# Row maximum subtracted on VectorE instead of GpSimd in a Swin block fused with a convolution block

## The chip, the cores and the metric

The kernel runs on one core of one Trainium2 chip. The metric is the device time of one launch in microseconds (us), the median of several runs. The engines of the core are TensorE (PE in the profile), VectorE (DVE), ScalarE (ACT), GpSimd (POOL) and SyncE (SP), which only issues DMAs here. Each works through its own instruction list in order; they meet through semaphores.

## The reference

Sixteen images of 128 channels x 32 x 32 pass through two blocks, all in float32. The first is a Swin block on 8x8 windows with 8 heads of 16 channels:

```
t    = layernorm(tokens)                    # per token, over 128 channels
q, k, v = t @ qkv_w.T + qkv_b               # 16 windows x 64 tokens, 8 heads
attn = softmax(q * scale @ k^T + bias)      # per window and head, 64 x 64, over the keys
tok  = tok + (attn @ v) @ proj_w.T + proj_b
out  = tok + gelu(layernorm(tok) @ w1.T + b1) @ w2.T + b2
```

The second is a convolution block on the output of the first: a 1x1 convolution with gelu, dilated row and column convolutions with 3x3 convolutions behind them, a pyramid of grouped 3x3 convolutions, an edge gate, a branch of 2D Fourier transforms, a softmax over five routes that mixes the branches, relu and a last 1x1 convolution.

The change concerns the softmax of the first block: `exp(s - max(s)) / sum`, where the maximum is over the 64 keys of one query and head.

## The kernel before

One call of `both(n, n+1)` on every engine computes the convolution block of image n and the Swin block of image n+1, interleaved. It is run 15 times: once for images 0 and 1, then 14 times in a loop. Ahead of it stands the Swin block of image 0 alone (`swin_rest(0)` on VectorE, `swin_only(0)` on GpSimd), behind it the convolution block of image 15 alone (`conv_only`). Nothing plans the order: it is the order of calls in each engine's list.

The attention of an image is done in 8 window pairs j = 0..7 (`PAIRS`). A pair's scores are a tile of 128 partitions (2 windows x 64 queries) by 512 columns (8 heads x 64 keys), in one of three `score` buffers. A pair goes through these steps:

1. PE, `scores` (L518): four matmuls per pair into PSUM bank 2 or 3.
2. DVE, `bias_max`: L957 adds the relative position bias and writes `score` to SBUF, L959 is a drain (wait until the engine's own work is written), L960 finds the 8 row maxima.
3. POOL, `less_max` (L1666): waits for the semaphore `s_max`, subtracts the maxima from `score` in place, 128x512, and signals `s_sub`.
4. ACT, `exponent` (L1382): waits for `s_sub`, exponential in place.
5. DVE, `row_sums`: L964 sums, L966 takes the reciprocal; POOL, `widen_inverse` (L1677), spreads the 8 inverse sums over 128 columns. PE, `prob_transposes` (L529), ACT, `prob_copy` (L1387), PE, `values` (L540).

On VectorE pair j+2 is prepared before pair j is summed, and a slot of convolution work follows each pair:

```
                bias_max(i, 0)
                route_logits(n)
                bias_max(i, 1)
                for j in range(PAIRS):
                    if j + 2 < PAIRS:
                        bias_max(i, j + 2)
                    row_sums(i, j)
```

So of the 8 calls of `bias_max`, two stand ahead of the loop and six in its passes j = 0 to 5. The convolution slots hold: j = 0 `mix_input` (L1129, L1131), j = 1 `odd_part` (L1032 to L1039), j = 2 and 3 taps (L1088, L1090) and the bias L1099, j = 4 `boosted` (L1108, L1113), j = 5 `even_product` (L1117), `odd_product` (L1124) and a tap, j = 6 `gate_pyramid` (L1139) and taps. In the pass j = 5 TensorE does `inverse_even` (L467, 16 matmul records), which waits for L1117, and then `pyramid_conv` (L647, 48 records), for which L1139 waits. All 8 calls of `bias_max` stand ahead of L1117 in VectorE's list.

GpSimd in `both` does `axis_conv` (L1696, L1706, L1708: taps of the row and column convolutions, with two of them in the passes j = 0 and 1), `residual_in` (L1660), `less_max`, `widen_inverse` and two additions at the end.

Of the kernel before, what the change touches and what calls it, by code (L numbers as in the profile page):

```python
# [27 lines left out]
ALU = mybir.AluOpType  # L28
ACT = mybir.ActivationFunctionType
AX = mybir.AxisListType  # L30
# [3 lines left out]
P = 128  # L34
CH = TOK // P
HALF = TOK // 2
WS, HEADS = 8, 8
WT = WS * WS
HD = C // HEADS
WIN = TOK // WT  # L40
PAIRS = WIN // 2
# [99 lines left out]
def swin_conv_kernel(nc, x, cols, rows, mats, cons, rel_index, out):  # L141
    with ExitStack() as ctx:
        def sb(name, *free, dt=F32):
            return ctx.enter_context(nc.sbuf_tensor(name, [P, *free], dt))

        def sem(name):
            return ctx.enter_context(nc.semaphore(name))
# [9 lines left out]
        def col(name, k=0):  # L157
            return cols_sb[:, COLS[name][0] + k:COLS[name][0] + k + 1]
# [40 lines left out]
        score = sb("score", 3, HEADS, WT)  # L199
# [3 lines left out]
        row_max, row_sum, row_inv = sb("row_max", 3, HEADS), sb("row_sum", 3, HEADS), sb("row_inv", PAIRS, HEADS)  # L203
# [52 lines left out]
        pool_turns = sem("pool_turns")  # L256
# [15 lines left out]
        v_sb = sem("v_sb")  # L272
        s_ps = sem("s_ps")
        s_biased = sem("s_biased")
        s_max = sem("s_max")
        s_sub = sem("s_sub")
        s_exp = sem("s_exp")
        s_inv = sem("s_inv")
# [85 lines left out]
        def grid(ap):  # L364
            return ap.rearrange("p (h w) -> p h w", w=SIDE)
# [545 lines left out]
        def _(dve):  # L911
# [40 lines left out]
            def bias_max(i, j):  # L952
                dve.wait_ge(s_ps, 8 * i + j + 1)
                if j >= 3:

                    dve.wait_ge(pT_ps, 8 * i + j - 2)
                dve.tensor_tensor(score[:, j % 3].rearrange("p h k -> p (h k)"), bank[2 + j % 2][:], rel_bias[:],  # L957
                                  ALU.add).then_inc(s_biased, 1)
                dve.drain()  # L959
                dve.tensor_reduce(row_max[:, j % 3], score[:, j % 3], AX.X, ALU.max).then_inc(s_max, 1)  # L960

            def row_sums(i, j):
                dve.wait_ge(s_exp, 8 * i + j + 1)
# [212 lines left out]
            def swin_rest(i):  # L1176
                keys(i)
# [6 lines that stand above are left out]
                scale_values(i, 0)  # L1184
                residual_stats(i, 0)
                scale_values(i, 1)
                norm2(i, 0)
                residual_stats(i, 1)
                norm2(i, 1)
                swin_out(i, 0)  # L1190
                swin_out(i, 1)
# [444 lines left out]
        @block.gpsimd  # L1636
        def _(pool):

            pool.memset(z_sb[:], 0.0)
            pool.drain()  # L1640
            pool.sem_inc(z_zeroed, 1)
            for padded in (hor, ver, pyr):
                pool.memset(padded[:], 0.0)
            pool.memset(v_pair[:], 0.0)
            pool.wait_ge(onehot_ready, 4)
            pool.memset(k_heads_flat[:, 0:WT * WT], 0.0)
            pool.wait_ge(rel_ps, 2)
            pool.memset(k_heads_flat[:, WT * WT:2 * WT * WT], 0.0)
            pool.drain()
            pool.sem_inc(zeroed, 1)  # L1650
            pool.wait_ge(setup_dve, 1)


            def residual_in(i):
                pool.wait_ge(xT_sb, 2 * i + 2)
                pool.sem_inc(pool_turns)

                pool.wait_ge(x1_sb, 2 * i)
                pool.sem_inc(pool_turns)
                pool.tensor_tensor(resT[:], xT[:], proj_shift[:].unsqueeze(1).broadcast_to([P, CH, C]), ALU.add)\  # L1660
                    .then_inc(res_sb, 1)

            def less_max(i, j):
                pool.wait_ge(s_max, 8 * i + j + 1)
                pool.sem_inc(pool_turns)
                pool.tensor_tensor(score[:, j % 3], score[:, j % 3],  # L1666
                                   row_max[:, j % 3].unsqueeze(2).broadcast_to([P, HEADS, WT]), ALU.subtract)\
                    .then_inc(s_sub, 1)

            def widen_inverse(i, j):  # L1670
                pool.wait_ge(s_inv, 8 * i + j + 1)
                pool.sem_inc(pool_turns)
                if j % 4 == 0:

                    pool.wait_ge(iv_ps, 2 * i)
                    pool.sem_inc(pool_turns)
                pool.tensor_copy(inv_wide[:, j], row_inv[:, j].unsqueeze(2).broadcast_to([P, HEADS, HD]))\  # L1677
                    .then_inc(iv_wide, 1)

            mid = AXIS_TAPS // 2  # L1680
            OFFSETS = [0] + [AXIS_DIL * (t - mid) for t in range(AXIS_TAPS)
                             if t != mid and abs(AXIS_DIL * (t - mid)) < SIDE]

            def axis_conv(n, a, offsets):

                dst, name = ((hor, "dilh"), (ver, "dilv"))[a]
                body = dst[:, 1:1 + SIDE, 1:1 + SIDE]
                for off in offsets:
                    weight = col(name, off // AXIS_DIL + mid)
                    if off == 0:  # L1690
                        pool.wait_ge(act_sb, 2 * n + 2)
                        pool.sem_inc(pool_turns)

                        pool.wait_ge(hv_sb, n)
                        pool.sem_inc(pool_turns)
                        pool.tensor_scalar(body, act_in, weight, 1.0, ALU.mult, ALU.mult)  # L1696
                        continue
                    lo, hi = max(0, -off), min(SIDE, SIDE - off)
                    if a == 0:
                        part = (slice(None), slice(None), slice(lo, hi))  # L1700
                        of = act_in[:, :, lo + off:hi + off]
                    else:
                        part = (slice(None), slice(lo, hi))
                        of = act_in[:, lo + off:hi + off]
                    pool.drain()
                    pool.tensor_scalar(axis_part[part], of, weight, 1.0, ALU.mult, ALU.mult)  # L1706
                    pool.drain()
                    last = pool.tensor_tensor(body[part], body[part], axis_part[part], ALU.add)  # L1708
                    if off == OFFSETS[-1]:
                        last.then_inc(axis_sb, 1)  # L1710

            def mix_pyramid(n):

                pool.wait_ge(py_sb, 2 * n + 2)
                pool.sem_inc(pool_turns)
                pool.wait_ge(xm_mixed, n + 1)
                pool.sem_inc(pool_turns)
                pool.tensor_tensor(py[:], py[:], grid(xm[:]), ALU.add).then_inc(pyramid_mixed, 1)

            def square_sum(n):  # L1720
                pool.wait_ge(be_sb, 2 * n + 2)
                pool.sem_inc(pool_turns)
                pool.wait_ge(bo_sb, 2 * n + 2)
                pool.sem_inc(pool_turns)
                pool.tensor_tensor(fa, fa, fb, ALU.add).then_inc(sq_sb, 1)

            def swin_only(i):
                residual_in(i)
                less_max(i, 0)
                less_max(i, 1)  # L1730
                for j in range(PAIRS):
                    if j + 2 < PAIRS:
                        less_max(i, j + 2)
                    widen_inverse(i, j)

            def both(n, i):
                axis_conv(n, 0, OFFSETS)
                axis_conv(n, 1, OFFSETS[:3])
                residual_in(i)
                less_max(i, 0)  # L1740
                less_max(i, 1)
                for j in range(PAIRS):
                    if j + 2 < PAIRS:
                        less_max(i, j + 2)
                    widen_inverse(i, j)
                    if j < 2:
                        axis_conv(n, 1, OFFSETS[3 + j:4 + j])
                mix_pyramid(n)
                square_sum(n)

            def conv_only(n):
                axis_conv(n, 0, OFFSETS)
                axis_conv(n, 1, OFFSETS)
                mix_pyramid(n)
                square_sum(n)

            swin_only(0)
            both(0, 1)
            with pool.Fori(1, IMAGES - 1) as n:
                both(n, n + 1)  # L1760
            conv_only(IMAGES - 1)
# [81 lines left out]
```

## Time and profile before

| | us |
|---|---|
| Median of 3 runs | 1808.63 (1806.32 to 1815.72) |
| The profiled execution's own time | 1805.41 |
| Its span in the trace | 1803.6 |
| PE busy | 1549.4 (86%) |
| DVE busy | 1364.0 (76%) |
| ACT busy | 864.2 (48%) |
| POOL busy | 684.9 (38%) |

Busy time of an engine is the sum of its instructions' durations; a matmul's end is modelled. Register, branch, semaphore and DMA-issuing instructions are not counted. "PEclk" is the clock that TensorE was granted, as a share of 2.4 GHz: 1.00 is 2.4 GHz, 0.50 is 1.2 GHz. The chain of waits is followed back from the last instruction: at each step to what released it, or to the instruction before it on its engine; "DVEq" is VectorE's queue, mostly its drains.

### The profile page before, as it was taken

Reading aid. Unit: us, or ns where it says so; the run is one execution under the profiler, and the core shown is the slowest. Engines: PE = TensorE matmul, PEld = TensorE weight load, DVE = VectorE, ACT = ScalarE, POOL = GpSimd, SP = SyncE. Lnnn points to the kernel's source line nnn. Section 1 sums busy time; section 2 is a strip of 40 time slices with the busy share of each in tenths; the row PEclk is TensorE's granted clock in tenths of the full one; section 3 lists DMA queues with packets and bytes.
Section 4 is the critical chain, followed back from the end, with each engine's and each line's share of the span. In section 5 each row is a group of like instructions: output and inputs, shape, how many; then the busy total and the mean of one; then the engine's idle time right before and its main releaser. Section 6 shows DMA issues by size and latency. Waiting matters only on the chain.

```text
span 1803.6 us, 32142 instructions
## 1 busy us (share of the span) xinstructions
PE 1549.4 (86%) x11664; PEld 906.3 (50%) x11664; DVE 1364.0 (76%) x2455; ACT 864.2 (48%) x1380; POOL 684.9 (38%) x603
## 2 busy tenths in 40 slices
PE   5789899888989889888998988889888898988884
PEld 3346455464555546445463554546455464555542
DVE  4558778687777878788687777868788786778866
ACT  2344545455454544545455454544545545454533
POOL 3244251634416244251534416134251623416151
PEclk9899999999999999999999999999999999999997
DMA  4011020111102011020111102011020201102020
GB/s 147 1 26 41 26 52 1 43 33 37 39 23 53 0 37 39 25 51 0 43 33 37 39 23 53 0 37 39 25 51 0 58 18 37 39 12 53 0 54 12
DMA packets 19618, 60.23 MB, mean 33 GB/s; under 512 B 6228, under 2 KB 6228, under 8 KB 19204
## 3 DMA queue, kind: packets, MB, share of 16 engines
q1 hardware_dynamic: 19588, 59.83, 13.7%
q8 instruction: 18, 0.29, 0.1%
q14 instruction: 12, 0.10, 0.0%
HBM read 14.04 MB, written 9.02 MB: 13 GB/s over the span
## 4 chain that ended last, share of the span: by engine, by line
DVE 39%; PE 25%; DVEq 16%; issue 7%; ACT 6%; SPq 4%; DMA 3%; ACTq 1%; POOL 0%; POOLq 0%
DVE hv L1090 16%; DVEq L959 7%; DVE nT L929 5%; PE bank L647 5%; PE bank L674 4%; SPq L428 4%; DVE row_max L960 4%; DVEq L965 3%; PE bank L467 3%; PE bank L518 3%; PE bank L489 2%; DMA k_heads<-kC 2%; PE bank L755 2%; DVE score L957 2%; PE bank L577 1%
## 5 line engine op out<-in xcount | busy, mean ns | idle before, releaser
L674 PE MATMUL bank<-act,mats_sb 128*32 128x512 f32 (+11 forms) x2112 | 267.1, 475 | 1.4 <-DVE xs L1026 1.4
L1666 POOL TENSOR_TENSOR score<-score,row_max 128x512 f32<-128x512 f32 x128 | 133.4, 1042 | 306.7 <-DVE row_max L960 305.1
L1350 ACT ACTIVATE fft<-bank 128x512 f32<-128x512 f32 x224 | 168.9, 807 | 125.7 <-PE bank L467 111.8
L1090 DVE SCALAR_TENSOR_TENSOR hv<-hor,mix,hv 128x1024 f32<-128x1024 f32 x128 | 193.8, 1514 | 10.7
L467 PE MATMUL bank<-cons_sb,fft 128*128 128x128 f32 x1280 | 185.4, 306 | 11.8 <-DVE fft L1117 11.8
L1090 DVE SCALAR_TENSOR_TENSOR hv<-ver,mix,hv 128x1024 f32<-128x1024 f32 x144 | 186.9, 1298 | 11.0
L1382 ACT ACTIVATE score<-score 128x512 f32<-128x512 f32 x128 | 80.8, 631 | 225.8 <-POOL score L1666 225.8
L467 PEld LDWEIGHTS bank<-cons_sb,fft 128*128 128x128 f32 x1280 | 172.7, 217 | 31.4 <-DVE fft L1117 17.0
L1677 POOL COPY inv_wide<-row_inv 128x128 f32<-128x128 f32 x128 | 91.8, 717 | 206.7 <-DVE row_inv L966 206.7
L674 PEld LDWEIGHTS bank<-act,mats_sb 128*32 128x32 f32 x2112 | 117.5, 109 | 99.6 <-issue 81.5
L1696 POOL TENSOR_SCALAR hor<-act,cols_sb 128x1024 f32<-128x1024 f32 x16 | 18.0, 1125 | 391.6 <-ACT act L1407 391.6
L518 PE MATMUL bank<-k_heads,qC 128*64 128x512 f32 x512 | 136.1, 621 | 31.8 <-DMA k_heads<-kC 31.8
L577 PE MATMUL bank<-nC,mats_sb 128*128 128x512 f32 x256 | 127.4, 621 | 38.9 <-ACT nC L1350 23.4
L957 DVE TENSOR_TENSOR score<-bank,rel_bias 128x512 f32<-128x512 f32 x128 | 87.2, 681 | 76.3 <-PE bank L518 76.2
L1387 ACT ACTIVATE probT<-bank 128x512 f32<-128x512 f32 x128 | 77.7, 607 | 101.6 <-PE bank L529 101.3
L1706 POOL TENSOR_SCALAR axis_part<-act,cols_sb 128x320 f32<-128x320 f32 (+1 forms) x128 | 109.4, 855 | 22.5 <-issue 22.5
L587 PE MATMUL bank<-fft,mats_sb 128*128 128x512 f32 x256 | 115.2, 593 | 0.0
L1400 ACT ACTIVATE fft<-bank,fold_b 128x512 f32<-128x512 f32 x128 | 79.2, 689 | 68.5 <-PE bank L577 68.5
L929 DVE TENSOR_SCALAR nT<-xT,mv,rstd 128x128 f32<-128x128 f32 x256 | 104.8, 491 | 3.8
L1708 POOL TENSOR_TENSOR ver<-ver,axis_part 128x320 f32<-128x320 f32 (+1 forms) x64 | 100.8, 1575 | 9.4
L960 DVE TENSOR_REDUCE row_max<-score 128x8 f32<-128x512 f32 x128 | 87.8, 686 | 11.6
L577 PEld LDWEIGHTS bank<-nC,mats_sb 128*128 128x128 f32 x256 | 45.1, 191 | 98.2 <-issue 34.4
(180 smaller groups left out, 2903.9 us busy)
## 6 DMA issues: line engine op xcount, KB each, us to landing
pyr_stack<-pyr SPq DMA_DIRECT2D x192, 144.2 KB, 3.1
x_in<-x_dram SPq DMA_DIRECT2D x16, 512.0 KB, 3.5
k_heads<-kC SPq DMA_DIRECT2D x128, 64.0 KB, 2.4
out_dram<-y_out SPq DMA_DIRECT2D x16, 512.0 KB, 2.8
k_heads<-rel_dram SPq DMA_DIRECT2D x2, 1024.0 KB, 13.0
mats_sb<-mats_dram SPq DMA_DIRECT2D x1, 1978.5 KB, 7.4
z_dram<-z_sb SPq DMA_DIRECT2D x32, 19.1 KB
z_run<-z_dram SPq DMA_DIRECT2D x16, 38.2 KB
```

Source lines behind the costliest of these rows:

```text
L467: last = pe.matmul(dst[:, c * P:(c + 1) * P], src[:, at:at + P], rhs, start=True, stop=True)
L518: last = pe.matmul(bank[2 + j % 2][64 * e:64 * e + 64, :], qC[:, w * WT:(w + 1) * WT], k_heads[:, :, w], start=True, stop=True)
L577: pe.matmul(bank[b][:], w_up[:, f * P:(f + 1) * P], nC[:, HALF * k:HALF * k + HALF], start=True, stop=True).then_inc(up_ps, 1)
L587: last = pe.matmul(bank[b][:], w_down[:, f * P:(f + 1) * P], hidden[:, f, HALF * k:HALF * k + HALF], start=False, stop=(f == FC - 1))
L674: last = pe.matmul(grids[32 * d:32 * d + 32, y0 - 16 * k:y1 - 16 * k, x0:x1], w_pyr[:, d, t], act[:, y0 + dy:y1 + dy, x0 + dx:x1 + dx], st ...
L929: last = dve.tensor_scalar(nT[:, c], source[:, c], mv[:, c, 0:1], rstd[:, c:c + 1], ALU.subtract, ALU.mult)
L957: dve.tensor_tensor(score[:, j % 3].rearrange("p h k -> p (h k)"), bank[2 + j % 2][:], rel_bias[:], ALU.add).then_inc(s_biased, 1)
L959: dve.drain()
L960: dve.tensor_reduce(row_max[:, j % 3], score[:, j % 3], AX.X, ALU.max).then_inc(s_max, 1)
L1090: last = dve.scalar_tensor_tensor(hv[:], src, mix[:, a, k:k + 1], hv[:], ALU.mult, ALU.add)
L1350: return act_.activation(dst, src, ACT.Copy)
L1666: pool.tensor_tensor(score[:, j % 3], score[:, j % 3], row_max[:, j % 3].unsqueeze(2).broadcast_to([P, HEADS, WT]), ALU.subtract)\
```

## The change

`bias_max` on VectorE gets a second drain and the subtraction behind the maximum. `less_max` on GpSimd and the semaphore `s_max` go. ScalarE's wait on `s_sub` stays as it is; it is now VectorE that raises it. No DMA, tile or matmul is touched.

```
@@ bias_max (VectorE)
                 dve.drain()
-                dve.tensor_reduce(row_max[:, j % 3], score[:, j % 3], AX.X, ALU.max).then_inc(s_max, 1)
+                dve.tensor_reduce(row_max[:, j % 3], score[:, j % 3], AX.X, ALU.max)
+                dve.drain()
+                dve.tensor_tensor(score[:, j % 3], score[:, j % 3],
+                                  row_max[:, j % 3].unsqueeze(2).broadcast_to([P, HEADS, WT]), ALU.subtract)\
+                   .then_inc(s_sub, 1)
@@ GpSimd
-            def less_max(i, j):
-                pool.wait_ge(s_max, 8 * i + j + 1)
-                pool.sem_inc(pool_turns)
-                pool.tensor_tensor(score[:, j % 3], score[:, j % 3],
-                                   row_max[:, j % 3].unsqueeze(2).broadcast_to([P, HEADS, WT]), ALU.subtract)\
-                    .then_inc(s_sub, 1)
@@ swin_only and both (GpSimd)
                 residual_in(i)
-                less_max(i, 0)
-                less_max(i, 1)
                 for j in range(PAIRS):
-                    if j + 2 < PAIRS:
-                        less_max(i, j + 2)
                     widen_inverse(i, j)
```

## Rows read from the trace of the kernel before

**Rows 1.** The page's chain that ended last, by engine and by line

```profile
DVE 39%; PE 25%; DVEq 16%; issue 7%; ACT 6%; SPq 4%; DMA 3%; ACTq 1%; POOL 0%; POOLq 0%
```

**Rows 2.** The chain in order of time, one attention stage: start us, us, what

```profile
920.65 1.36 DVE fft L1117
922.05 3.78 PE bank L467 x16
...
931.73 0.75 DVE py L1139
```

**Rows 3.** Timeline of DVE, same stage: start us, us, line, operation, [idle before]

```profile
887.72 0.87 DVE L1059 TENSOR_SCALAR route<-route,vec 128x5 f32<-128x5 f32 x1
...
889.27 0.69 DVE L960 TENSOR_REDUCE row_max<-score 128x8 f32<-128x512 f32 x1
892.09 0.69 DVE L957 TENSOR_TENSOR score<-bank,rel_bias 128x512 f32<-128x512 f32 x1 [2.13 <-PE bank L518]
892.87 0.69 DVE L960 TENSOR_REDUCE row_max<-score 128x8 f32<-128x512 f32 x1
893.47 0.68 DVE L964 TENSOR_REDUCE row_sum<-score 128x8 f32<-128x512 f32 x1
...
901.03 2.09 DVE L1032 TENSOR_TENSOR fft<-xs 128x930 f32<-128x930 f32 x1
...
910.62 2.70 DVE L1090 SCALAR_TENSOR_TENSOR hv<-hor,mix,hv 128x1024 f32<-128x1024 f32 x2
```

**Rows 4.** Timeline of POOL, same stage

```profile
919.88 1.04 POOL L1666 TENSOR_TENSOR score<-score,row_max 128x512 f32<-128x512 f32 x1 [2.53 <-DVE row_max L960]
```

**Rows 5.** DVE's groups by line and form: count, busy us, mean ns, idle before

```profile
L957 DVE TENSOR_TENSOR score<-bank,rel_bias 128x512 f32<-128x512 f32 x128 | 87.2, 681 | 76.3 <-PE bank L518 76.2
...
L1139 DVE SCALAR_TENSOR_TENSOR py<-bank,cols_sb,axis_part 128x512 f32<-128x512 f32 x32 | 24.0, 751 | 83.0 <-PE bank L647 83.0
...
L1159 DVE TENSOR_TENSOR hv<-hv,py 128x1024 f32<-128x1024 f32 x16 | 19.6, 1226 | 1.2
```

**Rows 6.** Single lines over the whole run: duration ns min/median/max

```profile
L1117 DVE TENSOR_TENSOR fft<-fft x16: 1226/1343/1348, 162.0 to 1759.1; 128x1024 f32<-128x1024 f32 x16
...
L1032 DVE TENSOR_TENSOR fft<-xs x32: 1859/2104/3014, 119.4 to 1747.2; 128x930 f32<-128x930 f32 x32
```

**Rows 7.** Waits of all engines: us in total, times, longest

```profile
ACT score L1382 <- POOL score L1666: 225.8, 113, 6.4
...
PEld bank L529 <- ACT score L1382: 27.0, 32, 1.8
```

**Rows 8.** Stretches: us, busy (x) of PE, PEld, DVE, ACT, POOL, PEclk, DMA share, GB/s

```profile
892.00:922.00 30.00, 26.72 (x234) 16.18 (x232) 27.96 (x44) 13.53 (x22) 17.27 (x16) 0.97 0.26 59
...
872.00:876.00 4.00, 4.00 (x11) 2.48 (x12) 0.45 (x1) 0.60 (x1) 3.52 (x5) 0.53 0.00 0
...
922.00:926.00 4.00, 3.95 (x20) 3.69 (x24) 3.37 (x5) 2.79 (x4) 0.35 (x2) 0.50 0.00 0
```

**Rows 9.** Timeline of PE behind L1117 in the next image of the loop

```profile
1029.50 3.55 PE L467 MATMUL bank<-cons_sb,fft 128*128 128x128 f32 x16 [1.04 <-DVE fft L1117]
1032.98 5.36 PE L647 MATMUL bank<-pyr_stack,mats_sb 96*32 96x512 f32 x48
...
1038.50 2.05 PE L467 MATMUL bank<-cons_sb,fft 128*128 128x128 f32 x16
```

**Rows 10.** Timeline of DVE, first image, Swin block alone

```profile
58.82 0.69 DVE L957 TENSOR_TENSOR score<-bank,rel_bias 128x512 f32<-128x512 f32 x1 [0.37 <-PE bank L518]
...
61.53 0.69 DVE L957 TENSOR_TENSOR score<-bank,rel_bias 128x512 f32<-128x512 f32 x1 [0.37 <-PE bank L518]
```

**Rows 11.** Timeline of DVE, the wait behind the first normalisation, in two images

```profile
875.55 0.75 DVE L949 TENSOR_SCALAR kC<-bank,fold_b 128x512 f32<-128x512 f32 x1 [3.73 <-PE bank L489]
877.16 0.75 DVE L949 TENSOR_SCALAR kC<-bank,fold_b 128x512 f32<-128x512 f32 x1 [0.86 <-PE bank L489]
...
983.82 1.52 DVE L949 TENSOR_SCALAR kC<-bank,fold_b 128x512 f32<-128x512 f32 x2 [2.33 <-PE bank L489]
```

More of the change, by code:

```diff
@@ L274, in swin_conv_kernel @@
         s_biased = sem("s_biased")
-        s_max = sem("s_max")
         s_sub = sem("s_sub")
@@ L1739, in both @@
                 residual_in(i)
-                less_max(i, 0)
-                less_max(i, 1)
                 for j in range(PAIRS):
-                    if j + 2 < PAIRS:
-                        less_max(i, j + 2)
                     widen_inverse(i, j)
```

## The prediction

> **What bounds the kernel now.** I read the chain that ended last, by engine, first. VectorE stands on it with 39%, its queue (drains behind its own work) with 16%, TensorE with 25%, and GpSimd with 0% [rows 1]. So work goes from an engine that is on no step of the chain to the one that is on most of it. The question is what of VectorE's own list is covered where the new work lands.
>
> For that I read the chain in order of time and the timelines in one pass of the loop, at 885 to 932 us. The reader is to see three parts. (a) Pairs 0 and 1 go through VectorE, which is done with the maximum of pair 1 at 889.27 + 0.69 = 889.96, and then idles 2.13 us until TensorE's scores of pair 2 let L957 start at 892.09 [rows 3]. (b) From 892.09 to L1117 at 920.65 VectorE has no wait for another engine of over 0.3 us: in 892 to 922 its instructions take 27.96 of 30 us, and the rest is the spacing of some 0.08 us at its drains. TensorE is busy 26.72 us of the same 30 and holds 0.97 of the full clock [rows 8]. (c) L1117 ends at 922.0, TensorE starts L467 on it at 922.05, and VectorE's L1139 waits for L647 until 931.73 (the second half; the first started 929.26) [rows 2]; these waits sum to 83.0 us in the run [rows 5]. What is late at L1117 is therefore late at the end of the image, because the chain goes from VectorE to TensorE and back without slack. From this L957 (pair 2, the last one that waits) to L1117 it is 920.65 - 892.09 = 28.56 us [rows 2, 3], and in all 15 passes between 28.4 and 28.6, whatever the clock did elsewhere. VectorE's own list sets this stage.
>
> **The change part by part.** The subtraction on VectorE, with both inputs in SBUF and 128x512 float32, is not in the trace. The nearest rows are L957, the same shape with one input in PSUM, 0.681 us on average, and L1159, both inputs in SBUF at 1024 columns, 1.226 us [rows 5]. Between the two lie 512 columns, (1.226 - 0.681) / 512 = 1.06 ns a column, which leaves 0.14 us fixed: 0.68 to 0.69 us for the new instruction. Lower bound: 0.61, half of L1159, as if nothing were fixed. Upper bound: L1032, whose inputs are read with large strides, takes at least 1.859 us for 930 columns [rows 6], 1.83 ns a column over the fixed 0.14, so 1.09 us if reading one maximum 64 times over were as slow as that. I take 0.69, since the second input is a contiguous stretch of 8 values, and nothing in the trace shows such a rate for a repeated value.
>
> The Trainium skill ("VectorE: DVE Perf Modes", the section on the errata) gives a float32 tensor_tensor add in SBUF as 691 ns at 512 columns; by that page the term would be the same, and no run here shows the exact instruction yet.
>
> It stands behind a drain. L960 to L964, with none between, start 893.47 - 892.87 = 0.60 apart; L957 to L960, with one, start 892.87 - 892.09 = 0.78 apart for a 0.69 instruction [rows 3]. New order: L960, 0.78 to the subtraction, 0.60 to L964; so 1.38 in place of 0.60, which adds 0.78 us a pair (0.70 to 1.18 with the bounds).
>
> Pairs 0 and 1 (part a): 2 x 0.78 = 1.56 us added. L1059, a 128x5 instruction, takes 0.87 us now, since GpSimd's subtraction of pair 0 runs beside it; its neighbour L1057 on as little data takes 0.16. That 0.65 us should come back. Net 0.9 us, against 2.13 us of idle time [rows 3]. Cost nothing, 1.2 us of cover left; at the upper bound 1.7 us, still covered. Were the cover gone it would cost 0.9 us a pass.
>
> Pairs 2 to 7 (part b): 6 x 0.78 = 4.68 us a pass on the path.
>
> What comes back in part b, because GpSimd's 1.04 us subtraction no longer runs beside VectorE: L1117 takes 1.343 as a median and 1.226 at least [rows 6], 0.12 us, and there L1666 runs from 919.88 to 920.92, over L1117's start [rows 4]. L1032 takes 2.09 against 1.86 undisturbed, 0.23 us [rows 3, 6]. The first of the two L1090 at 910.62 gives 0.06 (2.70 for two that take 1.28 each with 0.08 between) [rows 3]. Sum 0.41. The axis taps that GpSimd runs beside j = 0 and 1 shift with the inverse sums that release them and end, by the same shifts, about 0.1 us ahead of the new subtraction; up to 0.1 us a pass of loss if that fails, which I leave in the range.
>
> The Trainium skill ("SBUF — State Buffer", section "SBUF: two separate sides") says that GpSimd and VectorE share one pair of SBUF ports as an exclusive lock, held for a whole instruction, the other fully blocked. By that rule L1117, begun at 920.65 [rows 2], would lose the 0.27 us until 920.92 and not 0.12; taken so at all three places the return would be about 0.95 us a pass in place of 0.41, and the sum some 8 us lower. The trace shows less than half of the rule's price at L1117, and I go by it.
>
> ScalarE's exponential starts earlier by the difference of the hops: GpSimd's 1.04 plus some 0.2 of semaphores against 0.78. ScalarE waits 225.8 us for GpSimd's subtraction, but TensorE waits only 27.0 us for the exponential [rows 7], and VectorE's sums come two pairs later. Worth nothing in part b. GpSimd is free of 133 us of work that was on no step of the chain: nothing.
>
> Part c moves as a whole by 4.68 - 0.41 = 4.27 us. Fifteen passes: 64 us. The first image, alone: pairs follow each other at 61.53 - 58.82 = 2.71 us, of which VectorE idles 0.37 [rows 10], so 2.34 + 0.78 = 3.12 us of VectorE's work a pair exceeds the pace by 0.4; over some five pairs 2 us, between -2 (the shorter hop to the exponential) and +4. The last image has no softmax.
>
> Own time of the profiled execution 1805.4 (span 1803.6) + 64 + 2 = 1871. The median of three runs is 1808.6, 3 above the profiled one, the lowest 1 above; I take +1: 1872 us.
>
> The clock is the term that I can't work out. TensorE is granted 0.50 in 922 to 926 [rows 8], right behind three short waits on VectorE, and L467 then takes 3.78 us, in the next image 3.55, where 16 records take 2.05 at full clock [rows 9]. Over the 15 passes the time from L1117 to the first L1139 comes as 7.8, 9.1 and 8.6 us in turn, mean 8.5. There is a second such place: TensorE idles while VectorE normalises, the clock falls to 0.53 [rows 8], and VectorE then waits 3.73 + 0.86 = 4.59 us instead of 2.33 [rows 11]; that happens in one pass of three. A pass of 112 us and not 108 will meet this otherwise. If the clock never fell at either place: 15 x (1.7 at L467 + 0.5 at L647) + 5 x 2.26 = 44 us less. If it fell at both in every pass, as in the worst now: 15 x 0.6 + 10 x 2.26 = 32 us more. TensorE will idle more in part b, so I don't expect the good end.
>
> **The rivals.** (R1) *The clock turns against it.* VectorE feeds TensorE more slowly, TensorE's waits in part b grow from some 1 us to 1.8, and the clock falls inside the stage, where TensorE has 26.72 us of work in 30 [rows 8] and at half clock becomes the bound for some us. For it: so little reserve. Against: in 892 to 918 it holds 1.00 throughout. Price: the 32 us above, up to 1903; with a drop inside the stage of 1.7 us a pass, 1928. The Trainium skill ("TensorE: Matmul & The Clock Gate", "HAM oscillation — how this bites in real kernels") says that TensorE fed in bursts falls back to half clock again and again; the granted 0.50 behind the waits agrees.
>
> (R2) *The clock turns for it.* The longer pass puts the fall elsewhere, under VectorE's work. Price: 20 to 44 us less, 1828 to 1852.
>
> (R3) *Not slower.* The pace of the stage is not VectorE's work but the way from maximum to exponential to transposes, through GpSimd. The shorter hop would then win, at most the 27.0 us that TensorE waits for the exponential [rows 7], and the subtractions would fill VectorE's waits for scores, 76.2 us in the run [rows 5]: 1778 to 1806. It decides only if VectorE idles in part b for over 0.78 us a pair. Against it: those waits stand at pairs 0 to 2 and in the first image, and in part b there are none.
>
> (R4) *The repeated maximum is read slowly*: 1.09 us each, 6 x 0.40 x 15 = 36 us more, 1908.
>
> **How the numbers follow.** Forecast (1853 to 1888): 72%. R1 above that: 13%. R2 below that: 8%. R4: 4%. R3: 3%. All but R3 are slower. The likeliest case gives 1872; with a part of R1 and R2 the range is 1849 to 1899. A measurement of this kernel tells about 0.5%, 9 us, from no change: faster 0.02, same 0.02, slower 0.96.
>
> **What would show it.** The new line takes 0.69 us, 128 times; L960 to L964 start 1.38 apart; from pair 2's L957 to L1117 it takes 28.56 + 4.27 = 32.8 us in every pass; L957 of pair 2 still waits, for about 1.2 us; L1059 takes under 0.3 us, L1117 1.23; L1139 still waits some 5 us a pass; the last image is unchanged. It is wrong if pair 2's L957 to L1117 grows by less than 3 us, if the new instruction takes over 0.8, or if L1139 waits less by what L1117 is late.

## The result, and the profile after

| | before | after |
|---|---|---|
| Median, us | 1812.18 (4 runs) | 1881.91 (4 runs, 1877.05 to 1885.19) |
| Ratio, 95% interval | | 1.0383 [1.0337, 1.0429] |
| Profiled execution's own time / span, us | 1805.41 / 1803.6 | 1880.26 / 1878.4 |

The change makes the kernel 3.8% slower, 69 us by the ratio. The forecast was 1872 us, 66 above the profiled execution; that execution came out 74.8 us longer in span. Further runs of the kernel before, beside the experiments, brought its median to 1810.8 and 1812.7. The profiled execution of the kernel before, 1805.41 us, is faster than each of its 34 timed ones (1805.9 to 1820.62), while that of the kernel after lies near its median: so some 5 of the 74.8 us come from which executions are compared, and not from the change.

The page of the kernel after: busy time by engine, and the chain that ended last by engine. [rows 1] is the chain before.

```profile
PE 1583.0 (84%) x11664; PEld 927.6 (49%) x11664; DVE 1428.6 (76%) x2583; ACT 863.5 (46%) x1380; POOL 546.8 (29%) x475
...
DVE 41%; PE 27%; DVEq 14%; issue 6%; ACT 6%; SPq 4%; DMA 3%; ACTq 1%
```

GpSimd is 138 us less busy and VectorE 65 us more. GpSimd had 0% of the chain before, so what its relief is worth can only be what it gives back to VectorE's instructions.

The timeline of VectorE after, pairs 0, 1 and 2 of one pass (start us, us, line, operation, idle before); it answers to [rows 3]. L956, L959, L961 and L967 are bias, maximum, the new subtraction and the sum.

```profile
923.79 0.23 DVE L1062 TENSOR_SCALAR route<-route,vec 128x5 f32<-128x5 f32 x1
...
925.47 0.69 DVE L961 TENSOR_TENSOR score<-score,row_max 128x512 f32<-128x512 f32 x1
927.39 0.69 DVE L956 TENSOR_TENSOR score<-bank,rel_bias 128x512 f32<-128x512 f32 x1 [1.23 <-PE bank L517]
928.17 0.69 DVE L959 TENSOR_REDUCE row_max<-score 128x8 f32<-128x512 f32 x1
928.93 0.69 DVE L961 TENSOR_TENSOR score<-score,row_max 128x512 f32<-128x512 f32 x1
929.54 0.68 DVE L967 TENSOR_REDUCE row_sum<-score 128x8 f32<-128x512 f32 x1
...
937.85 1.72 DVE L1035 TENSOR_TENSOR fft<-xs 128x930 f32<-128x930 f32 x1
...
957.72 0.69 DVE L956 TENSOR_TENSOR score<-bank,rel_bias 128x512 f32<-128x512 f32 x1 [0.78 <-PE bank L517]
...
960.91 1.23 DVE L1120 TENSOR_TENSOR fft<-fft 128x1024 f32<-128x1024 f32 x1
```

What to see: maximum to sum now start 929.54 - 928.17 = 1.37 us apart, not 0.60; the wait ahead of pair 2's score has shrunk from 2.13 to 1.23 us; the route instruction L1062 takes 0.23 us and not 0.87; and there is a wait that wasn't there, 0.78 us ahead of pair 7's score at 957.72.

TensorE in the same pass, ahead of that wait and behind it:

```profile
947.56 0.66 PE L528 MATMUL bank<-cons_sb,score 128*128 128x128 f32 x4
951.92 3.75 PE L466 MATMUL bank<-mats_sb,fft 128*128 128x128 f32 x16 [3.70 <-DVE fft L1102]
955.60 0.66 PE L539 MATMUL bank<-probT,v_pair 128*32 128x64 f32 x16
956.18 1.49 PE L517 MATMUL bank<-k_heads,qC 128*64 128x512 f32 x4
...
962.20 3.79 PE L466 MATMUL bank<-cons_sb,fft 128*128 128x128 f32 x16 [2.03 <-DVE fft L1120]
```

The same place in the kernel before:

```profile
914.06 2.02 PE L467 MATMUL bank<-mats_sb,fft 128*128 128x128 f32 x16 [1.28 <-DVE fft L1099]
```

Stretches of the kernel after, with the granted clock (us, busy (x) of PE, PEld, DVE, ACT, POOL, then PEclk, DMA share, GB/s):

```profile
926.00:950.00 24.00, 21.35 (x193) 12.71 (x192) 21.02 (x35) 11.94 (x19) 9.78 (x8) 1.00 0.33 74
950.00:957.00 7.00, 5.08 (x34) 4.20 (x36) 6.61 (x11) 0.63 (x1) 0.29 (x1) 0.52 0.00 0
960.00:967.00 7.00, 4.97 (x26) 3.89 (x28) 5.35 (x8) 4.08 (x6) 1.59 (x2) 0.53 0.00 0
```

VectorE reaches L1102 later, TensorE waits 3.70 us and not 1.28, the clock falls to 1.2 GHz, the 16 records take 3.75 and not 2.02 us, and pair 7's scores (L517) come too late for VectorE. This is so beyond the one pass. In 14 of the 15 passes TensorE waits 3.66 to 3.86 us at L1102 and the 16 records take 2.54 to 3.76 us; in the last pass it waits 2.35 us and they take 2.02, as they do in all 15 passes of the kernel before, behind waits of 1.1 to 1.3 us. Pair 7's score is late, by 0.7 us or more, in the five passes in which they take 3.75 us or more.

The second place where the clock counts is behind the first normalisation. TensorE in two passes of the kernel after, a short and a long one:

```profile
909.43 0.66 PE L458 MATMUL bank<-cons_sb,nT 128*128 128x128 f32 x4 [1.80 <-DVE nT L928]
...
910.45 1.98 PE L488 MATMUL bank<-nC,mats_sb 128*128 128x512 f32 x4
...
1021.81 1.08 PE L458 MATMUL bank<-cons_sb,nT 128*128 128x128 f32 x4 [1.80 <-DVE nT L928]
...
1023.55 3.78 PE L488 MATMUL bank<-nC,mats_sb 128*128 128x512 f32 x4
```

The wait just ahead is 1.80 us in both, so its length alone does not decide. VectorE's wait at kC, which follows, is the long one in 9 passes of 15, where it was in 5.

**Where the 74.8 us are.** From the VectorE timelines of all 15 passes, before against after:

| stretch of a pass | before, us | after, us | over 15 passes |
|---|---|---|---|
| pair 2's score to the even product, passes without a wait at pair 7 | 28.4 to 28.6 | 32.65 to 32.9 | +62.3 (15 x 4.15) |
| the same, what late passes add | none | 5 passes with a wait at pair 7, 0.7 to 1.3; one late through GpSimd, 1.4 | +6.0 |
| pass begin to pair 2's score | 27.7, 28.7 in the first, 29.9 to 30.3 in 5 | 27.7, and 29.7 to 30.3 in 9 | +8.9 |
| even product to first L1142 | 7.7 to 9.1, mean 8.47 | 7.5 to 8.9, mean 8.27 | -3.0 |
| Swin block of the first image | | | +0.9 |

The sum is 75.1 us against 74.8 in span; so 62 us are VectorE's work, some 10 us TensorE's clock (4.6 at pair 7, 8.9 ahead of pair 2, less 3.0), 1.4 GpSimd and 0.9 the first image. The stage's 62 us are there in every trace of a kernel with the six subtractions (32.6 to 33.0 us in its undisturbed passes); the clock's share is less certain. In the profiled executions of the runs with pairs 0 and 1 alone and with nobody subtracting (below), whose medians are that of the kernel before, the wait behind the first normalisation is the long one in 8 and in 7 passes. So part of the step from 5 to 9 can be chance, and by the medians, 69 to 70 us apart, the clock costs nearer 5 us than 10.

The pass that is late through GpSimd shows how the two engines delay each other, and what it costs when the order turns. VectorE's `mix_input` and GpSimd's tap start within 0.05 us of each other in all 15 passes. In the pass of the rows above VectorE comes through undisturbed and GpSimd waits; VectorE, then GpSimd:

```profile
931.27 1.28 DVE L1132 SCALAR_TENSOR_TENSOR xm<-act,mix,xm 128x1024 f32<-128x1024 f32 x1
932.62 2.30 DVE L1134 SCALAR_TENSOR_TENSOR xm<-xs,mix,xm 128x1024 f32<-128x1024 f32 x1
```

```profile
931.24 1.92 POOL L1703 TENSOR_SCALAR axis_part<-act,cols_sb 128x672 f32<-128x672 f32 x1 [0.19 <-issue]
```

In the one late pass, the last of the loop, it is the other way round, and VectorE pays 0.58 + 0.72 us:

```profile
1721.64 1.86 DVE L1132 SCALAR_TENSOR_TENSOR xm<-act,mix,xm 128x1024 f32<-128x1024 f32 x1
1723.58 3.02 DVE L1134 SCALAR_TENSOR_TENSOR xm<-xs,mix,xm 128x1024 f32<-128x1024 f32 x1
```

```profile
1721.60 0.83 POOL L1703 TENSOR_SCALAR axis_part<-act,cols_sb 128x672 f32<-128x672 f32 x1 [0.19 <-issue]
```

### The profile page after: what moved, and what is told of

Its sections match the earlier page's. It is cut to its first block, busy times and chain, and to the rows that moved or that the text cites. A ratio compares the mean times of both kernels' runs of the same rounds, so it can differ in the third digit from the quotient of the medians.

```text
span 1878.4 us, 32142 instructions
## 1 busy us (share of the span) xinstructions
PE 1583.0 (84%) x11664; PEld 927.6 (49%) x11664; DVE 1428.6 (76%) x2583; ACT 863.5 (46%) x1380; POOL 546.8 (29%) x475
## 4 chain that ended last, share of the span: by engine, by line
DVE 41%; PE 27%; DVEq 14%; issue 6%; ACT 6%; SPq 4%; DMA 3%; ACTq 1%
DVE hv L1093 16%; DVEq L958 6%; PE bank L466 5%; DVE nT L928 5%; PE bank L646 5%; PE bank L673 4%; PE bank L517 4%; SPq L427 4%; DVE score L961 3%; DVE row_max L959 3%; DVEq L968 3%; PE bank L488 2%; DMA k_heads<-kC 2%; PE bank L754 2%; DVE score L956 2%
## 5 line engine op out<-in xcount | busy, mean ns | idle before, releaser
L1385 ACT ACTIVATE score<-score 128x512 f32<-128x512 f32 x128 | 80.8, 631 | 269.0 <-DVE score L961 269.0
L517 PE MATMUL bank<-k_heads,qC 128*64 128x512 f32 x512 | 143.0, 650 | 28.9 <-DMA k_heads<-kC 28.9
L956 DVE TENSOR_TENSOR score<-bank,rel_bias 128x512 f32<-128x512 f32 x128 | 87.6, 685 | 71.3 <-PE bank L517 71.2
L466 PE MATMUL bank<-mats_sb,fft 128*128 128x128 f32 x512 | 84.2, 332 | 56.9 <-DVE fft L1102 56.9
L466 PEld LDWEIGHTS bank<-mats_sb,fft 128*128 128x128 f32 x512 | 77.9, 240 | 73.8 <-issue 73.8
L959 DVE TENSOR_REDUCE row_max<-score 128x8 f32<-128x512 f32 x128 | 87.8, 686 | 11.7
```

Source lines behind the costliest of these rows:

```text
L466: last = pe.matmul(dst[:, c * P:(c + 1) * P], src[:, at:at + P], rhs, start=True, stop=True)
L517: last = pe.matmul(bank[2 + j % 2][64 * e:64 * e + 64, :], qC[:, w * WT:(w + 1) * WT], k_heads[:, :, w], start=True, stop=True)
```

## The experiments

All are edits of the kernel before or after; the ratio is to the kernel before, with its 95% interval.

**Pairs 0 and 1 alone.** VectorE subtracts for them, GpSimd for the other six; the two calls of `less_max` for pairs 0 and 1 go, and its wait counts six a pass.

```
+                if j < 2:
+                    dve.drain()
+                    dve.tensor_tensor(score[:, j % 3], score[:, j % 3], <row_max, broadcast>, ALU.subtract)\
+                       .then_inc(s_sub, 1)
...
```

> Only pairs 0 and 1 are subtracted on VectorE, pairs 2 to 7 stay on GpSimd. Theory (cover): VectorE idles 2.13 us ahead of pair 2's score in every pass, the two subtractions add 1.55 and L1059 gives 0.65 back, so about 1.2 us of idle time are left and the time stays: within 5 us of the kernel before. From pair 2's score to L1117 it takes 28.6 us as before. Rival (each subtraction costs the same wherever it stands): a quarter of the 70 us of the change, 17 us more.

Measured: 1815.43 us, 1.0015 [0.9996, 1.0034]. Within the expected 5 us. Pair 2's score to the even product takes 28.5 to 28.8 us, 28.57 on average, as in the kernel before. The timeline of VectorE in it, pair 1 and pair 2:

```profile
1003.83 0.69 DVE L963 TENSOR_TENSOR score<-score,row_max 128x512 f32<-128x512 f32 x1
1005.76 0.69 DVE L957 TENSOR_TENSOR score<-bank,rel_bias 128x512 f32<-128x512 f32 x1 [1.23 <-PE bank L518]
```

Two of the eight subtractions are free: they lie in idle time of which 1.23 us is left. An equal price per pair, 17 us, is outside the interval.

**Pairs 2 to 7 alone.** The mirror image (`if j >= 2`), with a semaphore of its own for GpSimd's two.

> Only pairs 2 to 7 are subtracted on VectorE, pairs 0 and 1 stay on GpSimd. Theory (place): this holds the whole cost of the change, 6 x 0.77 us less some 0.5 us given back by GpSimd's absence, 62 us over 15 passes, and the clock's part, so 62 to 76 us over the kernel before; pair 2's score to L1117 takes 32.7 us or more, L1059 stays at 0.87 us. Rival (equal cost per pair): three quarters of the change, 52 us.

Measured: 1884.34 us, 1.0428 [1.0376, 1.0481], 77 us by the ratio, a little over the 62 to 76 expected and clear of 52. Pair 2's score to the even product takes 32.76 to 32.8 us in the nine undisturbed passes. The whole cost stands here; its interval overlaps that of the whole change.

**Nobody subtracts.** The kernel before without `less_max`; the maximum is still found, and the exponential takes the raw scores.

> The kernel before, and nobody subtracts the maximum (it is still found; the exponential takes the raw scores). This leaves VectorE's list as before and only takes GpSimd's subtraction away, so it measures alone what its absence gives VectorE back. Theory: 0.5 us a pass (L1032 0.38, L1117 0.12, the first L1090 0.05), pair 2's score to L1117 28.0 us, L1059 0.23 us but hidden: 1 to 12 us faster than the kernel before. Rival (the whole port lock is given back, also at widen_inverse and the taps): 1 us or more a pass, over 15 us faster.

Measured: 1812.84 us, 0.9987 [0.9961, 1.0012]; pair 2's score to the even product 28.03 us in nearly all passes. L1117 and L1032 over the whole run, duration ns min/median/max:

```profile
L1117 DVE TENSOR_TENSOR fft<-fft x16: 1224/1225/1226, 163.5 to 1754.4; 128x1024 f32<-128x1024 f32 x16
...
L1032 DVE TENSOR_TENSOR fft<-xs x32: 1724/1836/3793, 121.5 to 1742.5; 128x930 f32<-128x930 f32 x32
```

GpSimd's absence is worth 28.57 - 28.03 = 0.54 us a pass by the trace, 8 us in all. The time doesn't show it: 8 us less would be 0.9956, just outside the interval. In the profiled execution 7 us go lost again ahead of pair 2's score, where the long wait comes in 7 passes and not 5. The rival of 15 us and more is out. What this run wins is the most that the change could have won, since here nobody does the work at all.

**GpSimd busy beside it.** The changed kernel, with GpSimd subtracting on scratch tiles as often as before.

```
+            def less_max(i, j):
+                pool.wait_ge(s_max, 8 * i + j + 1)
+                pool.sem_inc(pool_turns)
+                pool.drain()
+                pool.tensor_tensor(spare4[:], spare3[:], <spare8, broadcast>, ALU.subtract)
```

> The changed kernel, and GpSimd again does a 128x512 subtraction per pair, released by the maximum as before, but on scratch tiles nobody reads. Theory: VectorE's own subtraction has the shared port first (it starts 0.08 us behind the maximum, GpSimd some 0.2), GpSimd's copy waits and then runs 0.7 us later than in the kernel before, over the sums and the start of the convolution slot: VectorE loses the 0.5 us a pass again, up to 1 us, 5 to 15 us over the changed kernel. Rival (GpSimd's hold of the port delays VectorE's subtraction itself): it takes over 1 us, 15 x 6 x 0.4 = 36 us or more.

Measured: 1882.4 us, 1.0386 [1.036, 1.0411], where the changed kernel has 1.0383; the 5 to 15 us expected on top don't show, though the intervals are too wide to rule 5 out. Pair 2's score to the even product takes 32.9 us, 0.2 more than in the changed kernel and less than the 0.5 expected. VectorE's subtraction keeps its 0.69 us in all 128 cases, so the rival is out; the other side pays, and so do VectorE's small instructions behind it. That loss is at pairs 0 and 1, where it only shortens the wait for pair 2's score, from 1.23 to 0.35 us. Of this kernel, VectorE's first route instruction (0.15 us when undisturbed) and, below, GpSimd's scratch subtraction:

```profile
931.10 1.01 DVE L1062 SCALAR_TENSOR_TENSOR route<-route,base 128x5 f32<-128x5 f32 x1
```

```profile
930.65 1.44 POOL L1676 TENSOR_TENSOR spare<-spare 128x512 f32<-128x512 f32 x1 [7.46 <-DVE row_max L963]
```

1.44 us and not 1.04: it waits some 0.4 us of the time until VectorE's subtraction ends, at 931.18. In the stage VectorE loses 0.2 us a pass to its neighbour, against the 4.15 of the change.

**Twice.** The changed kernel with one more subtraction, of zeros, per pair.

```
+                dve.drain()
+                dve.tensor_tensor(flat, flat, spare[:], ALU.subtract).then_inc(s_sub, 1)
```

> The changed kernel, and VectorE subtracts a tile of zeros once more from each pair's scores, behind another drain (same result). Theory: 6 x 0.77 us a pass in the stage and 1.54 - 1.23 = 0.31 at pair 2, whose idle time is then used up, 74 us over 15 passes, and some 5 us in the first image: 75 to 85 us over the changed kernel, 150 over the one before; pair 2's score waits no more. Rival (clock): TensorE is starved further, its clock falls more often inside the stage and each pass pays 1 to 2 us on top: over 95 us.

Measured: 1943.46 us, 1.0736 [1.0651, 1.0822]: 133 us over before, 64 over the change, less than expected. Its stage takes 37.2 us in the undisturbed passes, 4.5 more than the change's, close to 6 x 0.77; pair 2's score waits no more, as expected. So the price of an instruction is right and linear in the stage. Four passes take 38.5 to 38.7 us, late by the same turned order at `mix_input` (1.86 and 3.03 to 3.05 us for its two instructions). The clock took less here in the passes, not more: in the profiled execution the wait behind the first normalisation is the long one in 5 passes of 15, where the change has 9, and the wait at pair 7 is gone. That execution, at 1950.66 us, lies 7 above its median, and the four timings lie 28 us apart, so the 64 us are rough.

**The same work elsewhere.** The kernel before with six scratch subtractions between the second normalisation and the last nine taps.

```
+                for _ in range(6):
+                    dve.drain()
+                    dve.tensor_tensor(spare[:], spare[:], rel_bias[:], ALU.subtract)
```

> The kernel before with six 128x512 float32 subtractions on a scratch tile on VectorE, each behind a drain, between the second normalisation and the last nine taps, outside the attention stage. Same work as the six subtractions on the path, at another place. Theory: the price of VectorE's work is the same there (6 x 0.77 x 15 = 69 us), but nothing is given back by GpSimd and TensorE's clock doesn't fall inside the attention stage: pair 2's score to L1117 stays 28.6 us in every pass, no wait at pair 7's score. 62 to 75 us over the kernel before. Rival (the taps have slack, so what is late there is hidden): under 20 us. On the clock: if the slow passes at kC come from the length of the pass alone, their number changes from 5 of 15 here too; if they come from the attention stage, it stays 5.

Measured: 1961.8 us, 1.0827 [1.0794, 1.086], twice what was expected: 150 us for 4.6 us of work a pass. By the profiles the passes are 9.7 us longer each, and 7 us more come ahead of the first pass, where nothing was added but the granted clock is 0.76 and not 0.99 (80 to 105 us). The attention stage is untouched, 28.4 to 28.6 us, and no pass waits at pair 7. The trace of VectorE shows the six at their price, and the wait for the next image's first activation grown from 4.96 to 6.76 us:

```profile
1144.54 4.52 DVE L1224 TENSOR_TENSOR spare<-spare,rel_bias 128x512 f32<-128x512 f32 x6
...
1173.65 0.21 DVE L1003 TENSOR_SCALAR vec<-sums 128x1 f32<-128x1 f32 x1 [6.76 <-ACT act L1412]
```

TensorE waits longer while VectorE finishes its taps:

```profile
1166.56 3.78 PE L756 MATMUL bank<-fft,mats_sb 128*128 128x512 f32 x4 [5.96 <-ACT fft L1526]
1170.13 2.12 PE L608 MATMUL bank<-xm,mats_sb 128*128 128x512 f32 x4
...
1185.24 1.12 PE L460 MATMUL bank<-cons_sb,nT 128*128 128x128 f32 x4 [1.97 <-DVE nT L931]
...
1187.02 3.78 PE L490 MATMUL bank<-nC,mats_sb 128*128 128x512 f32 x4
```

In the kernel before, the last convolution's four records take half of that:

```profile
966.50 1.98 PE L755 MATMUL bank<-fft,mats_sb 128*128 128x512 f32 x4 [1.35 <-ACT fft L1521]
```

After 5.96 us of idle time the clock is at 1.2 GHz for L756, and again for L490 behind the normalisation, now in all passes. The 9.7 us of a pass are 4.6 of work, 1.8 at L756 and 3.3 between the pass's begin and pair 2's score (31.8 us on average, 28.55 before). The question on the clock has an answer in part: the passes with a long wait behind the first normalisation (over 25 us from the pass's begin to the route logits' first step) went from 5 to 15 of 15 without a change in the attention stage, so they don't need one. That it is the idle time of TensorE, and where in the pass it falls, fits all runs here; no run tests it against the length of the pass.

**Filler on TensorE.** The changed kernel; the transposes of pairs 4 and 5 are repeated while TensorE would wait.

```
-                    prob_transposes(i, j)
+                    prob_transposes(i, j, {4: 6, 5: 4}.get(j, 1))
```

> The changed kernel, and in each pass of the loop TensorE repeats the transposes of pair 4 (6 times in all) and of pair 5 (4 times), ahead of the waits for L1102 (bias of r_even) and L1120 (even product), with the same result: no VectorE work is changed, only TensorE's idle time in the stage is filled. Theory (clock): the fall to 1.2 GHz at these two places is from TensorE's idle time; with it filled, pair 7's score no longer comes late (6 us over 15 passes), L466 behind L1120 takes 2.05 us and the first L1142 comes 6.9 to 7.3 us after L1120 and not 8.3: 15 to 27 us faster than the changed kernel. Rival: the clock falls all the same, or the filler delays the copies; no gain or up to 15 us slower.

Measured: 1874.68 us, 1.036 [1.0317, 1.0403], against 1.0383 of the change. That is 4 us, within both intervals, and below the 15 to 27 expected. In one pass of the profiled execution:

```profile
944.10 2.02 PE L466 MATMUL bank<-mats_sb,fft 128*128 128x128 f32 x16 [1.67 <-DVE fft L1102]
...
949.25 3.61 PE L636 MATMUL bank<-z_run,ones 9*128 9x512 f32 x4 [1.76 <-DVE fft L1116]
952.80 3.64 PE L528 MATMUL bank<-cons_sb,score 128*128 128x128 f32 x16
956.26 1.96 PE L466 MATMUL bank<-cons_sb,fft 128*128 128x128 f32 x16
```

The first place keeps the clock, with its wait cut from 3.70 to 1.67 us. It does so in all 15 passes: waits of 1.5 to 1.7 us, 2.02 us for the 16 records, and no wait ahead of pair 7's score, where the change had one in 5 passes. So this fall comes from TensorE's idle time. The stage is late in 2 passes only, by the turned order at `mix_input`. But there is a new wait of 1.76 us at L636, and the clock falls there: the even product to the first L1142 takes 7.8 us on average, not 8.3, but between 6.2 and 8.9. Filling two of three gaps moves the fall in most passes. That the clock's share can be had back this way is not shown by the medians.

**Bias, maximum and subtraction in fewer steps.** The kernel before; one VectorE instruction adds the bias, negates and keeps the minimum of the row, and ScalarE's exponential takes scale -1 and that minimum as its bias. The shift is the maximum over the 8 heads of a query, which cancels in each head's softmax as well, as long as no head's scores lie so far below another's that its exponentials vanish.

```
+                dve.tensor_tensor_reduce(<score j>, bank[2 + j % 2][:], rel_bias[:], -1.0, 3e38,
+                                         ALU.add, ALU.min, accum_out=low[:, j % 3:j % 3 + 1]).then_inc(s_biased, 1)
...
+                act_.activation(<score j>, <score j>, ACT.Exp, bias=low[:, j % 3:j % 3 + 1], scale=-1.0)
```

> The kernel before, with bias and maximum in one VectorE instruction (add, times -1, minimum over the whole row as accumulator), and the subtraction in ScalarE's exponential (scale -1, the minimum as its bias). The shift is the maximum over all 8 heads of a query and not over one, which cancels in the softmax. GpSimd has no subtraction. Theory: VectorE loses the 0.69 us maximum and a drain for pairs 2 to 7, 6 x 0.6 to 0.78 us a pass, and gets 0.5 back; but TensorE has 26.7 us of work in the stage, so it becomes the bound: pair 2's score to L1117 25 to 26.5 us, 30 to 60 us faster than the kernel before. Rival (accumulating instruction costs as much as both): no change.

Measured: 1741.74 us, 0.962 [0.9595, 0.9645]: 3.8% faster than the kernel before and 7% faster than the change. Over the upper end of what was expected. The line over the whole run (duration ns min/median/max) and VectorE in one pass:

```profile
L958 DVE CUSTOM_DVE_ANT_0 score<-bank,rel_bias x128: 664/691/698, 48.2 to 1596.0; 128x512 f32<-128x512 f32 x128
L958 DVE DVE_READ_ACCUMULATOR2_ANT low<- x128: 71/82/101, 48.8 to 1596.6; 128x1 f32 x128
```

```profile
855.50 0.69 DVE L958 CUSTOM_DVE_ANT_0 score<-bank,rel_bias 128x512 f32<-128x512 f32 x1 [4.16 <-PE bank L518]
856.11 0.08 DVE L958 DVE_READ_ACCUMULATOR2_ANT low<- 128x1 f32 x1
856.11 0.68 DVE L964 TENSOR_REDUCE row_sum<-score 128x8 f32<-128x512 f32 x1
...
870.17 0.69 DVE L958 CUSTOM_DVE_ANT_0 score<-bank,rel_bias 128x512 f32<-128x512 f32 x1 [1.26 <-PE bank L518]
...
881.10 1.23 DVE L1117 TENSOR_TENSOR fft<-fft 128x1024 f32<-128x1024 f32 x1
```

The maximum costs nothing beside the addition. Pair 2's score to L1117 is 25.6 us (28.56 before), with VectorE now waiting for TensorE at pair 7 in every pass (0.6 us) and at pair 5 in seven (1.2 to 1.3). In the other eight `mix_input` has the turned order, and they take the same 25.6 us: in the stage TensorE is the bound, as expected. The rest is the clock. TensorE is fed without long gaps, L467 behind L1117 takes 2.05 us, and L1117 to the first L1139 6.21 us in every pass, where it had been 7.7 to 9.1; only the first pass meets the long wait at kC. The profiled execution is the fastest of the five, 1725.57 us and 16 below the median, at the same granted clock as the median one (0.972 and 0.971); what the others lose is not known.

## Why the prediction was right, and where it was off

- **GpSimd on no step of the chain, VectorE's list the bound between pair 2 and L1117.** Right where it matters: the chain has GpSimd's subtraction three times, 3 us, all in the first image. Before, the stretch was the same in all passes; afterwards it grew by 4.15 us in the nine undisturbed ones, 4.27 was the estimate. "In every pass" did not come true: six took 0.7 to 1.4 us longer.
- **Price of the subtraction.** 0.69 us estimated, median 0.692. The bounds were not needed, and the rival of a slowly read maximum (R4) is out.
- **Spacing.** 1.38 us from maximum to sum estimated, 1.37 measured. Six times 0.77 is 4.62.
- **Pairs 0 and 1 free.** Right, by the run with these alone. 1.23 us of idle time is left, as said; L1059 gave back 0.64 of its 0.87 us.
- **What comes back.** 0.41 us a pass estimated; 4.62 - 4.15 = 0.47 in the changed kernel and 0.54 with nobody subtracting. The term at L1032 was 0.37 and not 0.23. The port rule of the Trainium skill ("SBUF — State Buffer", "SBUF: two separate sides"), priced at 0.95 us, overstated it (0.27, 0.43 and 0.25 us of overlap cost 0.12, 0.37 and 0.06); its direction holds: the run with GpSimd busy shows either engine waiting for the other.
- **Exponential earlier, worth nothing.** Right as far as it goes: ScalarE's wait for the subtraction even grew, from 225.8 to 269.0 us, without a use for it either way.
- **First image.** +2 estimated, +0.9 measured, which the clock's changes there can hide: the run with the work late in the pass, whose first image has no added work but a lower clock, begins its first pass 7 us later.
- **The clock.** This is the term left at nothing in the sum, and in the profile its 10 us are the 9 between forecast and span. A part of R1 happened: it fell inside the stage, at a wait that had grown by 2.4 us, and not at a TensorE that was out of reserve. R1 had TensorE's waits growing from some 1 us to 1.8; they grew from 1.28 to 3.70 at L1102 and to 2.03 at L1120. The sizes are with the table of the result: +4.6, +8.9 and -3.0. "In 892 to 918 it holds 1.00" was weak evidence against it, because the change lengthens exactly the waits that follow that stretch. What would have helped is to work out how long each TensorE wait in the stage becomes: five subtractions, pairs 2 to 6, stand ahead of L1116 of the kernel after and four ahead of L1102, so the wait of 1.28 us at the latter had to grow by 4 x 0.77 less what TensorE's own list was delayed, some 2 to 3 us.
- **R3, not slower.** Out: with the exponential released earlier and nobody subtracting the time doesn't change, so the hop through GpSimd sets no pace.
- **The base.** The forecast of the median took the kernel before as only 1 us above its profiled execution. With the median of the later runs, 1810.8 to 1812.7, it is 5 to 7, and the same sum would have given 1877 to 1879, against 1881.9. So the 10 us between 1872 and the median are about half the base and half the clock.

That the measured time lies inside the range is the mechanism's doing for its 62 us; that the clock's part came out so small is luck in part, since the prediction could not work it out and priced it anywhere from -44 to +57 us.

What is open: how the clock's cost comes about pass by pass. Six more instructions on VectorE, some 4.6 us a pass, cost 5 us a pass as pairs 2 to 7 alone, and 10 late in the pass; the doubled subtraction cost 4.3. The records' durations show the clock at these places; the amounts weren't predictable from any row.

## What to carry to other kernels

Moving work off a relaxed engine onto the one whose list bounds the stage costs its full start-to-start price, drain included, for every instance that has no idle time in front of the next wait; count the instances inside and outside the bounded stretch, and test the split by moving each part alone. What the relieved neighbour gives back was a ninth of the price here. The clock of TensorE is a term of its own: work out how long each of its waits becomes, and compare medians and not one execution with another before a few us are put down to it. Before moving a step, ask whether it can be folded into instructions that run anyway: the accumulator of the addition and the bias of the exponential made both the maximum and the subtraction disappear.

## What the runs showed of the hardware that was not expected

- The price of VectorE work depends on what TensorE does meanwhile: 4.5 us of it behind the second normalisation cost 10 us a pass; TensorE then idled 4.3 to 6.0 us and ran its next four 512-column records in 3.78 us and not 1.98, and the later L490 likewise.
- A wait of TensorE of 1.67 to 1.76 us was followed by full clock at one place and by half clock at another in the same pass of the filler run, and the same wait of 1.80 us in the kernel after by either.
- VectorE's `mix_input` and GpSimd's tap, which start within 0.05 us of each other, are served in one order in 14 passes and in the other in one (in four with the doubled subtraction, in eight in the fused kernel, in none before); the other order costs VectorE 1.3 us.
- An accumulating addition on VectorE (128x512, one input in PSUM) takes 0.691 us, against 0.681 for the plain one, and 0.082 for the read of the accumulator, which overlaps: the next instruction starts 0.61 us behind, as after a plain one without a drain.
